# Shared-key attention in a chain of eight sublayers: the causal mask as a bf16 product into the score banks

## What is computed

```
h = _ln(x, ln1_g, ln1_b)
q = (h @ wq + bq).reshape(B, S, N_HEADS, HEAD_DIM)
kv = h @ wkv + bkv
k, v = (kv[..., :KV_DIM], kv[..., KV_DIM:])
scores = jnp.einsum('bshd,btd->bhst', q, k) * scale
causal = jnp.tril(jnp.ones((S, S), bool))
scores = jnp.where(causal, scores, jnp.finfo(scores.dtype).min)
probs = jax.nn.softmax(scores, axis=-1)
attn = jnp.einsum('bhst,btd->bshd', probs, v).reshape(B, S, H)
x = attn @ wo + bo + res
h = _ln(x, ln2_g, ln2_b)
h = jax.nn.gelu(h @ wfc + bfc, approximate=True)
return h @ wproj + bproj + res
```

## Time and profile before

| | before |
|---|---|
| median of 3 executions | 2623.26 us (2620.5 to 2629.05) |
| profiled execution: its time | 2626.29 us |
| profiled execution: span, first to last instruction | 2624.5 us |
| the phase `l3_attn` in it | 2002.7 to 2400 us |
| mean granted TensorE clock over the span | 0.932 of full speed |
| busy share of the span | PE 86%, VectorE 65%, ScalarE 55%, GpSimd 30% |

### The profile page before, as it was taken

How to read it: one execution, slowest core, us unless ns; L and a number is a source line. 1 busy time by engine, 2 the same in 40 slices (tenths; PEclk the granted TensorE clock), 3 DMA queues, 4 the chain that set the end, 5 groups by cost and what they waited for, 6 DMA issues and landing times. The chain is left out here.

```text
span 2624.5 us, 48418 instructions
## 1 busy us (share of the span) xinstructions
PE 2247.6 (86%) x15901; PEld 1944.7 (74%) x15909; DVE 1699.0 (65%) x4091; ACT 1443.6 (55%) x3765; POOL 789.0 (30%) x808
## 2 busy tenths in 40 slices
PE   6997878999999949999389889998686899987997
PEld 5875777999999939998166667767585566666886
DVE  4675776888787855552379888777465575663443
ACT  4664456777777713333377666775333565663332
POOL 1111000011111120000658777778484222221000
PEclk9888998999999969999689999999797999998999
DMA  4000111000000483332411111000300000000000
GB/s 131 1 0 13 45 54 33 1 18 18 18 18 18 103 223 114 119 103 86 130 41 49 50 47 43 33 34 1 115 0 1 1 1 0 0 0 1 1 0 32
DMA packets 98856, 111.40 MB, mean 42 GB/s; under 512 B 32330, under 2 KB 87235, under 8 KB 97621
## 3 DMA queue, kind: packets, MB, share of 16 engines
q1 hardware_dynamic: 91156, 87.23, 11.0%
q0 software_dynamic: 7488, 21.50, 2.6%
HBM read 79.73 MB, written 28.97 MB: 41 GB/s over the span
## 5 line engine op out<-in xcount | busy, mean ns | idle before, releaser
L1863 POOL TENSOR_TENSOR l2a_hb<-l2a_hb,l2a_Cb 128x1024 f32<-128x1024 f32 x128 | 303.1, 2379 | 112.9 <-DVE l2a_hb L2319 111.8
L2319 DVE TENSOR_TENSOR_SCAN l2a_hb<-l2a_dA,l2a_dB 128x1024 f32<-128x1024 f32 x128 | 288.3, 2274 | 62.6 <-PE l2a_dB L1944 26.8
L2173 ACT ACTIVATE l2a_dA<-l2a_delta,l2a_An 128x255 f32<-128x255 f32 x512 | 214.3, 497 | 37.3 <-DVE l2a_delta L2259 20.9
L1944 PE MATMUL l2a_dB<-l2a_diag,l2a_dxT 64*128 64x128 f32 x2048 | 188.8, 306 | 31.2 <-DVE l2a_hb L2319 18.4
L1944 PEld LDWEIGHTS l2a_dB<-l2a_diag,l2a_dxT 64*128 64x128 f32 x2048 | 139.8, 194 | 95.1 <-PE l2a_dB L1944 37.2
L903 PE MATMUL l1a_QK<-l1a_xh,early_wqkv_h 128*128 128x256 f32 x512 | 147.6, 288 | 11.1 <-issue 9.6
L903 PE MATMUL l1a_QK<-l1a_xh,early_wqkv 128*128 128x256 f32 x512 | 144.9, 283 | 0.0
L903 PE MATMUL l1a_QK<-l1a_xl,early_wqkv_h 128*128 128x256 f32 x512 | 144.8, 283 | 0.0
L1964 PE MATMUL l2a_YS<-ident,l2a_hb 128*128 128x128 f32 x1024 | 142.4, 286 | 1.0 <-POOL l2a_hb L1863 1.0
L1174 ACT ACTIVATE l1a_ex<-l1a_S,l1a_nm 128x256 f32<-128x256 f32 x256 | 119.3, 471 | 36.2 <-DVE l1a_nm L1226 36.2
L1964 PEld LDWEIGHTS l2a_YS<-ident,l2a_hb 128*128 128x128 f32 x1024 | 116.8, 146 | 12.2 <-POOL l2a_hb L1863 1.2
(11 more groups left out here) (657 smaller groups left out, 7427.3 us busy)
## 6 DMA issues: line engine op xcount, KB each, us to landing
l2a_Cb<-c_rows SPq DMA_DIRECT2D x8, 2048.0 KB, 7.0
l1f_xl<-moe_x_rows SPq DMA_DIRECT2D x95, 128.0 KB, 2.0
moe_y_rows<-l1f_yo SPq DMA_DIRECT2D x95, 128.0 KB, 1.7
l0f_raw<-in_L_attn_w_qkv_dram SPq DMA_DIRECT2D x24, 256.0 KB, 2.9
moe_x_rows<-X SPq DMA_DIRECT2D x1, 4224.0 KB, 17.3
l1f_dL<-in_L_ffn_Wd_dram SPq DMA_DIRECT2D x1, 3072.0 KB, 22.1
X<-in_L_attn_x_dram SPq DMA_DIRECT2D x8, 256.0 KB, 6.1
routes_raw<-in_L_attn_w_o_dram SPq DMA_DIRECT2D x4, 512.0 KB, 3.9
```

Source lines behind the costliest of these rows:

```text
L1863: nc.gpsimd.tensor_tensor(h[:, :, :], h[:, :, :], Cb[p][:, s0:s0 + UN, :], ALU.mult).then_inc(hc_ready, 1)
L1944: last = nc.tensor.matmul(out[:, m:m + 2, j * P + a:j * P + a + HP], dxT[q][a:a + HP, j, c * P:(c + 1) * P], diag[q][a:a + HP, j, s0 + m:s ...
L2173: last = nc.scalar.activation(dA[(i * NU + u) % DAS][:, n, 1:SEQ], delta[q][:, c, 1:SEQ], ACT.Exp, scale=An[:, c, s0 + n:s0 + n + 1])
L2319: nc.vector.tensor_tensor_scan(flat(hb[u % RING]), flat(dA[(i * NU + u) % DAS]), dB[u % 2][:, :], 0.0, ALU.mult, ALU.add).then_inc(scanned, 1)
```

## The change

The mask is no longer added by VectorE. GpSimd makes a bf16 copy of the 128 x 128 mask, four times side by side (`hide4`), and a bf16 identity (`identb`). `scores` first issues, for each of its two banks, the product identity x mask into the last 128 key columns of each head (`start=True`), and the score products then accumulate on top (`start=False`). VectorE's maxima and ScalarE's exponentials read the bank itself. The tile `sm` and the semaphore `masked` are gone, and a bank is released by `exp_ready`, the end of its block's exponentials.

```diff
-        hide = ph.sb("hide", [P, 2 * P])
+        hide = ph.sb("hide", [P, P])
+        hide4 = ph.sb("hide4", [P, 4, P], BF16)
+        identb = ph.sb("identb", [P, P], BF16)
...
-        sm = ph.sb("sm", [P, NB, 512])
...
+            pool.wait_ge(masks_ready, 3)
+            nc.gpsimd.tensor_copy(hide4[:, :, :], hide[:, None, :].to_broadcast([P, 4, P])).then_inc(masks_ready, 1)
+            nc.gpsimd.tensor_copy(identb[:, :], ph.ident[:, :]).then_inc(masks_ready, 1)
             nc.gpsimd.memset(v1[:, :, :, HD:2 * HD], 1.0).then_inc(ones_ready, 1)
             rsqrt(pool, var1_ready, eps1_added, rstd1_ready, mv1, vp1, rs1, 0)
...
             pe.wait_ge(wkr_ready, 1)
+            pe.wait_ge(masks_ready, 5)
             queries(pe, 0, 0)
...
                 if b >= 3:
-                    pe.wait_ge(masked, done(b - 3))
+                    pe.wait_ge(exp_ready, done(b - 3))
                 if b >= 2:
-                    pe.wait_ge(masked, done(b - 2))
+                    pe.wait_ge(exp_ready, done(b - 2))
+                for g in (b, b + 1):
+                    _, _, nh, keys_n = ST[g]
+                    own = S[g % 3][:, :].rearrange("p (n k) -> p n k", n=nh)[:, :, keys_n - P:keys_n]
+                    nc.tensor.matmul(own, identb[:, :], hide4[:, 0:nh, :], start=True, stop=False, skip_group_check=True)
...
-                                                kz[rows, h % HC, 0:keys_n], start=True, stop=True)
+                                                kz[rows, h % HC, 0:keys_n], start=False, stop=(n == nh - 1), skip_group_check=True)
...
-                            last = nc.scalar.activation(ex[:, b % NB, cols], sm[:, b % NB, cols], ACT.Exp, bias=nm[:, b % NB, n:n + 1])
+                            last = nc.scalar.activation(ex[:, b % NB, cols], S[b % 3][:, cols], ACT.Exp, bias=nm[:, b % NB, n:n + 1])
...
-                    m = sm[:, b % NB].rearrange("p (h k) -> p h k", h=nh)
-                    nc.vector.tensor_tensor(m, S[b % 3][:, :].rearrange("p (h k) -> p h k", h=nh),
-                                            hide[:, None, 2 * P - keys_n:2 * P].to_broadcast([P, nh, keys_n]), ALU.add
-                                            ).then_inc(masked, 1)
-                    dve.wait_ge(masked, done(b))
-                    nc.vector.tensor_reduce(mx[:, b % NB, 0:nh], m, AX_X, ALU.max).then_inc(max_ready, 1)
+                    nc.vector.tensor_reduce(mx[:, b % NB, 0:nh], S[b % 3][:, :].rearrange("p (h k) -> p h k", h=nh), AX_X, ALU.max
+                                            ).then_inc(max_ready, 1)
```

More of the change, by code:

```diff
@@ L2602, in l3_attn @@
         (masks_cleared, masks_ready, stats1_ready, var1_ready, eps1_added, rstd1_ready,
-         q_ready, kv_ready, q_kept, k_kept, v_kept, kz_ready, s_ready, masked, max_ready, nm_ready, exp_ready, e_turned,
+         q_ready, kv_ready, q_kept, k_kept, v_kept, kz_ready, s_ready, max_ready, nm_ready, exp_ready, e_turned,
          eT_kept, pv_ready, rz_ready, av_kept, back0, back1, at0_ready, ones_ready, at_ready, at_turned, atT_kept, y2_ready, xb_ready, r1_ready, stats2_ready,
@@ L2607, in l3_attn @@
             "masks_cleared masks_ready stats1_ready var1_ready eps1_added rstd1_ready q_ready kv_ready "
-            "q_kept k_kept v_kept kz_ready s_ready masked max_ready nm_ready exp_ready e_turned eT_kept pv_ready rz_ready "
+            "q_kept k_kept v_kept kz_ready s_ready max_ready nm_ready exp_ready e_turned eT_kept pv_ready rz_ready "
             "av_kept back0 back1 at0_ready ones_ready at_ready at_turned atT_kept y2_ready xb_ready r1_ready stats2_ready var2_ready eps2_added rstd2_ready n2_ready "
@@ L2663, in _ @@
             pool.wait_ge(masks_cleared, 2)
-            nc.gpsimd.affine_select(out=hide[:, P:2 * P], in_=hide[:, P:2 * P], compare_op=ALU.is_ge, fill=-BIG, base=0,
+            nc.gpsimd.affine_select(out=hide[:, :], in_=hide[:, :], compare_op=ALU.is_ge, fill=-BIG, base=0,
                                     pattern=[[-1, P]], channel_multiplier=1).then_inc(masks_ready, 1)
@@ L2672, in _ @@
                                     pattern=[[HD, HC]], channel_multiplier=-1).then_inc(masks_ready, 1)
+            pool.wait_ge(masks_ready, 3)
+            nc.gpsimd.tensor_copy(hide4[:, :, :], hide[:, None, :].to_broadcast([P, 4, P])).then_inc(masks_ready, 1)
+            nc.gpsimd.tensor_copy(identb[:, :], ph.ident[:, :]).then_inc(masks_ready, 1)
             nc.gpsimd.memset(v1[:, :, :, HD:2 * HD], 1.0).then_inc(ones_ready, 1)
             rsqrt(pool, var1_ready, eps1_added, rstd1_ready, mv1, vp1, rs1, 0)
-            pool.wait_ge(masks_ready, 3)
+            pool.wait_ge(masks_ready, 5)
             pool.wait_ge(l3a_loaded, late.L3A)
```

## The result

| | before | after |
|---|---|---|
| median of 20 executions each, same chip | 2626.55 us | 2634.51 us |
| profiled span | 2624.5 us | 2630.7 us |
| the phase `l3_attn` in it | 396.82 us | 403.22 us |
| the rest of the span | 2227.7 us | 2227.5 us |
| one item of the loop (mean of five) | 45.14 us | 45.97 us |

The ratio is 1.003 with an interval of 1.002 to 1.0039: 5 to 10 us slower. In the two profiled executions all of it lies in the changed phase. The item period is read from GpSimd's `kz` products, one per item, from the fourth to the ninth. In the kernel after, GpSimd's timeline has

A forecast was written before the change was run, and what follows sets the result against it. PE sets the pace, with some waits between its blocks. Masks +13.9, half clock +0.9, casts +0.8, gain at S8 -7.0, items 0 and 1 -2.8: +5.8, rounded +6, median 2629.3 us, range 2620 to 2640.

The forecast's parts named there:

- The masks' columns: Two bf16 mask products per `scores` call on PE, 0.22 or 0.11 us each: +1.74 us per item, +13.9 in all.
- The gain at S8: Less PE waiting around S8, PT6 and `back0`: gross gain 0.88 us per item, -7.0 over 8 items.
- Who is late next: ScalarE: S8 must wait for E6, behind C4 and `h2T`; masks at +2.99, S8 at +3.30 us from PT4.
- `queries` still waits 1.6: PE's 1.60 us wait before `queries`, for ScalarE's `xT` behind PT8 and C8, was to stay unchanged.
- Reading PSUM: Maxima and exponentials read from the bank: nothing for maxima, 0.03 us gained per exponential, 0.4 in all, inside the rounding.
- Start and end of the phase: Start, items 0 and 1: half clock +0.9, casts +0.8, fewer waits on VectorE -2.8 us; no separate end term.
- casts: GpSimd's two casts before the first item's reciprocal root delay everything in item 0: +0.8 us.
- The four waits at 0.72 each: Two VectorE passes between PE and ScalarE saved in each of items 0 and 1: -2.8 us, between 0 and -6.
- The clock: Item 0 starts at half clock, where the products of S0 and S2 cost 0.43 each instead of 0.22: +0.9 us.
- the dearer mask block: Rival, chance 0.19: mask block costs 0.19 us per call beyond its columns, 9.1 more: +15, 2638 us.
- The late release: Rival, chance 0.17: banks freed at the exponential make S4 and S6 wait, 1.0 us per item, 8 in all: 2637.
- The further relief: Rival, chance 0.14: VectorE's relief also shortens the wait before `queries`; half gone gives -3, all gone -10 us, 2613.

The follow-up runs named there:

- e1: The changed kernel without its two mask products per call (attention not causal): item 44.10 us, ratio 0.9969 to the kernel before.
- e3: The changed kernel with ScalarE's `h2T` moved from before E6 to behind `av0`: item 45.19 us, ratio 1.0008 to the kernel before.
- f1: The kernel before with ScalarE's `xT` moved from behind C8 to behind E8: item 43.28 us, ratio 0.9931 to the kernel before.
- e4: The changed kernel with ScalarE's `xT` moved from behind C8 to behind E8: item 44.10 us, ratio 0.9967 to the kernel before.
- f3: The changed kernel without products or casts, VectorE adding the mask in the bank, `h2T` and `xT` both moved: item 43.13 us, ratio 0.994 to before.

## Why the prediction came out as it did

The time (+5.8 forecast for the profiled execution, rounded to +6; +6.2 in its span and +8.0 in the medians) and the mechanism both held. Point by point:

- **The masks' columns**: 0.22 and 0.11 from start to start, 1.74 per item; the trace after has steps of 0.22 and of 0.11 to 0.12. The whole price measured 1.87 (e1): at S8 the change to half rows had been hidden in the wait and is now behind the masks, 0.1 more. The prediction has this 0.09, but in its count of S8's position (+3.30), so it stands there in the gain and not in the price. Booked as e1 books it, the forecast price is 1.74 + 0.09 = 1.83.
- **The gain at S8**: 0.88 per item, or 0.97 booked in the same way. Measured 1.04 (e1), net of the 0.22 that S8's new wait takes. So the two misses are 0.04 and 0.07, and they partly cancel: +0.86 forecast, +0.83 measured.
- **Who is late next**: E6 behind C4 and `h2T`. All positions from PT4 came within 0.11, and e3 shows that taking `h2T` from the front of E6 removes the wait.
- **`queries` still waits 1.6**: yes, 1.60. f1 and e4 show that the wait comes from the place of `xT` in ScalarE's list.
- **Reading PSUM**: exponentials 504 to 486 ns, where 33 less was shown by another phase; an E of two takes 0.85 in place of 0.91. From the start of one exponential to the next the gain is 0.04, more than their own length shows (rows below). Maxima 686 to 689 ns, so nothing, as taken. The Trainium skill (VectorE: DVE Perf Modes, "The TRN2 errata — SBUF-src ops pay a fixed extra latency per instruction") would have 62 cycles more for the maxima from PSUM; the trace does not show them. For ScalarE it would have 52 cycles less, which the prediction put at 0.04 us; the step from one exponential to the next agrees with that, while their own length is only 18 ns less.
- **Start and end of the phase**: here the sum's parts were off by 0.5 and 0.4. Up to the third item's `kz` the kernel after is 1.1 late; forecast for items 0 and 1 together +0.6 (masks 3.5, clock 0.9, casts 0.8, gains -1.8 and -2.8). The four waits at 0.72 each were an estimate, and this part of it was not taken apart beyond the casts. Nor can these two traces do it, since the clock differs in them (rows below), and that the start came out near its forecast may be in part luck. At the end there is a 49th call of `scores`: the trace has 98 weight loads of the mask product, since `begin` also runs for an item past the last. It costs 0.4 behind the ninth `kz` (42.55 against 42.11). The sum then reads 1.1 + 6 x 0.81 + 0.44 = +6.4.
- **The clock**: the half clock at the start was forecast from the earlier trace rows. The stretch from 2003 to 2037 shows 0.69 where it showed 0.64, both between the levels of 1.2 and 2.4 GHz; its part of the 1.1 was not measured by itself.

The exponentials in steps, by the rows of an E of four (ScalarE's timeline, before and below it after):

```profile
2197.96 1.28 ACT L2936 ACTIVATE l3a_ex<-l3a_sm,l3a_nm 128x128 f32<-128x128 f32 x4
```

```profile
2201.12 1.15 ACT L2945 ACTIVATE l3a_ex<-l3a_S,l3a_nm 128x128 f32<-128x128 f32 x4
```

The mean length of one of these goes from 391 to 380 ns, 0.01 of the 0.13. The other 0.12 is shared by the three steps from one start to the next: 0.04 each.

The clock from 15 to 84 us into the phase, before and below it after (columns of the earlier trace rows):

```profile
2017.73:2086.73 69.00, 56.73 (x368) 36.75 (x368) 47.52 (x109) 40.38 (x97) 13.68 (x19) 0.88 0.00 1
```

```profile
2017.32:2086.32 69.00, 55.25 (x381) 35.81 (x384) 31.14 (x83) 38.50 (x97) 13.84 (x18) 0.93 0.00 1
```

e3 had 0.89 there, and although its items are shorter than those of the kernel after, its third `kz` comes 0.4 later in the phase (85.28 against 84.88). So the +1.1 may hide a larger cost behind the better clock.

The rivals: the dearer mask block falls with 1.87 in place of 1.74 + 6 x 0.19 = 2.9. The late release is half right: S8 does wait for E6, as forecast, but S4 and S6 don't wait in the changed kernel; f3 shows the condition under which S6 does. The further relief falls: VectorE has no part in the wait before `queries`.

And one thing neither the change nor the prediction looked for: the same phase was 15.7 us shorter (396.82 to 381.08) with one call moved in ScalarE's list, while the change itself put more work on the busiest engine. Once the order is right, the change is a draw per item (43.28 against 43.32) and no gain over the whole execution, and moving only the eight cheap masks of an item gives the shortest item.

## What to carry to other kernels

Work taken off an engine that is not the bound is worth only the waits that it ends (here 1.04 of 8.9 us), and what it puts on the bounding engine is paid in full where that engine does not wait (1.87 for 1.74 of columns; 1.54 and 1.35 where some of it fell into waits), so compare those two first. A buffer whose release moves from the first reader to the last can make the writer wait for everything queued in front of that last reader; look at that queue, and move from it what isn't urgent. Price such a move in the list it will live in: `h2T` behind `av0` gains 0.78 us with one VectorE pass per block and loses 0.65 with two.

## What the runs showed of the hardware

- The idle time before a TensorE row undercounts what the wait costs: `queries` shows 1.60, and removing the wait gave 1.87 in one kernel and 1.86 in the other. Undisturbed, a row starts before the modelled end of the one ahead (0.50 behind PT8, whose row is 0.66 long), and the idle time is counted only from that end; the row behind the wait is also longer (1.99 against 1.89). The shorter waits of the earlier trace rows show the same: 0.54, 0.73 and 0.30 of idle time for 0.60, 0.81 and 0.45 of delay.
- Going from an fp32 product of 128 rows to one of 64 rows shows about 0.1 us, and it is paid once per change whether the full-array product ahead is fp32 or bf16 (0.31 from the mask to S10's scores, 0.22 of it columns). It hid in a wait that stood directly ahead of the half-row product, and no longer does where the mask stands between them (S8, 0.32).
- A maximum over 512 fp32 columns took 689 ns from a PSUM bank and 686 from SBUF; an exponential over 256 columns 486 ns from a bank and 504 from SBUF, and an E of four exponentials over 128 columns 1.15 us in place of 1.28, so 0.04 less from one to the next.
